# Layer 0's expert rows sorted over four batches instead of two, with raw rows loaded again and a new order of the work

## The reference, cut to what matters

```
xn = _layernorm(x)
x = x + _L0_attn_ref(xn, ...) + _L0_ffn_ref(xn, ...)     # layer 0
xn = _layernorm(x)
x = x + _L1_attn_ref(xn, ...) + _L1_ffn_ref(xn, ...)     # layer 1
```

```
logits = xf @ gate_w; scores = softmax(logits); top_scores, top_idx = top_k(scores, 2)
xs = scale.T[:, :, None] * xf[None]
h = silu(einsum('etd,edh->eth', xs, w1)) * einsum('etd,edh->eth', xs, w3)
out = einsum('eth,ehd->etd', h, w2).sum(axis=0)
```

## Time and profile before

| what | value |
|---|---|
| runs | 1793.97 us median of 3 (1791.5, 1793.97, 1795.19) |
| profiled execution, first to last instruction | 1782.7 us, 11.3 us less than the median run |
| of it layer 0 (to the barrier at 569.6 us) | 569.6 us |
| of it layer 1 | 1213.1 us |
| TensorE matmul busy, whole program | 1631.9 us (92%) |
| VectorE / ScalarE / GpSimd busy | 1494.5 (84%) / 1330.3 (75%) / 1353.8 (76%) us |
| DMA, whole program | 139 GB/s mean |

### The profile page before, as it was taken

The page is one execution under the profiler, slowest core; times in us unless marked ns, Lnnn a source line. Parts: engine busy times, 40 slices in busy tenths (PEclk is TensorE's granted clock), DMA queues, the critical chain, the costliest instruction groups (busy, mean ns, idle before and its releaser), DMA issues.

```text
span 1782.7 us, 44372 instructions
## 1 busy us (share of the span) xinstructions
PE 1631.9 (92%) x13580; PEld 1005.0 (56%) x13580; DVE 1494.5 (84%) x2798; ACT 1330.3 (75%) x3259; POOL 1353.8 (76%) x1114
## 2 busy tenths in 40 slices
PE   6999899899884888799999999999999999999988
PEld 4576585685673354355456456456556555544645
DVE  6848758668565999989989999999989999998997
ACT  4867666666652867968978987888897897797765
POOL 2807707618634078998999899899899999889996
PEclk9999999999996989999999999999999999999999
DMA  9446445645465843374373455446535446445430
GB/s 283 153 131 139 141 141 140 163 148 122 132 177 135 218 139 94 109 202 107 121 195 95 143 137 131 126 133 149 150 105 147 121 124 175 102 143 155 113 95 25
DMA packets 164993, 247.65 MB, mean 139 GB/s; under 512 B 30776, under 2 KB 109304, under 8 KB 164760
## 3 DMA queue, kind: packets, MB, share of 16 engines
q1 hardware_dynamic: 152472, 228.02, 45.9%
q0 software_dynamic: 12288, 16.79, 4.6%
HBM read 168.08 MB, written 73.50 MB: 136 GB/s over the span
## 4 chain that ended last, share of the span: by engine, by line
PE 31%; DVE 11%; issue 9%; ACT 8%; POOL 6%; DMA 2%; SPq 1%; DVEq 0%; POOLq 0%; ACTq 0%
PE bank L2323 28%; POOL HB L2274 3%; DVE bank L2846 3%; PE bank L2423 3%; DVE HB L2846 2%; POOL HB L2280 2%; DVE SU L2818 2%; ACT bank L2636 1%; ACT PR L2674 1%; DVE HB L2851 1%; ACT PT L2558 1%; DVE rows L2793 1%; DMA BC<-ssm_scratch 1%; ACT PR L2667 1%; PE bank L2451 1%
## 5 line engine op out<-in xcount | busy, mean ns | idle before, releaser
L2274 POOL TENSOR_TENSOR HB<-DD,BC 128x512 f32<-128x512 f32 x512 | 642.0, 1282 | 98.7 <-DMA DD<-SU 45.7
L2636 ACT ACTIVATE bank<-DD,A 128x512 f32<-128x512 f32 x512 | 349.6, 694 | 116.7 <-DVE HB L2851 74.2
L2280 POOL TENSOR_TENSOR HB<-HB,BC 128x512 f32<-128x512 f32 x256 | 324.9, 1285 | 31.2 <-DVE HB L2846 29.8
L2846 DVE TENSOR_TENSOR_SCAN bank<-bank,HB 128x512 f32<-128x512 f32 x256 | 310.7, 1214 | 23.5 <-ACT bank L2636 18.0
L2846 DVE TENSOR_TENSOR_SCAN HB<-bank,HB 128x512 f32<-128x512 f32 x256 | 309.8, 1210 | 7.8 <-ACT bank L2636 4.6
L2851 DVE TENSOR_TENSOR HB<-bank,BC 128x512 f32<-128x512 f32 x256 | 175.1, 684 | 15.9 <-DVE bank L2846 0.9
L692 POOL DMA_INDIRECT X<-expert_out_scratch,slot x64 | 111.1, 1736 | 66.2 <-DMA expert_out_scratch<-YS 39.4
L2323 PE MATMUL bank<-HB,fold 128*32 128x512 f32 x1024 | 137.0, 607 | 22.4 <-POOL HB L2280 10.9
L2423 PEld LDWEIGHTS bank<-ident,PR 128*128 128x128 f32 x768 | 86.7, 142 | 83.4 <-issue 44.9
L2423 PE MATMUL bank<-ident,PR 128*128 128x128 f32 x768 | 114.6, 281 | 18.8 <-ACT PR L2674 7.4
L2323 PE MATMUL bank<-XT,edge 128*128 128x512 f32 x256 | 122.7, 613 | 2.2 <-ACT XT L2558 2.0
(11 more groups left out here) (286 smaller groups left out, 3584.1 us busy)
## 6 DMA issues: line engine op xcount, KB each, us to landing
DD<-dd_scratch SPq DMA_DIRECT2D x488, 128.0 KB, 3.2
ROW<-row_scratch SPq DMA_DIRECT2D x64, 256.0 KB
BC<-ssm_scratch SPq DMA_DIRECT2D x128, 128.0 KB, 3.9
US<-us_scratch SPq DMA_DIRECT2D x32, 512.0 KB, 4.9
dd_scratch<-SU SPq DMA_DIRECT2D x16, 1024.0 KB, 5.5
us_scratch<-SU SPq DMA_DIRECT2D x15, 1024.0 KB, 6.5
XL<-sorted_scratch SPq DMA_DIRECT2D x92, 128.0 KB, 2.4
expert_out_scratch<-YS SPq DMA_DIRECT2D x92, 128.0 KB, 1.8
```

The costliest lines, as they stand in the source:

```text
L2274: done(pool.tensor_tensor(HB[:, c % HR], du, bc, ALU.mult), "dbu")
L2280: done(pool.tensor_tensor(h, h, bc, ALU.mult), "cg")
L2636: done(act.activation(PD[n % 2][:], delta, ACT.Exp, scale=A[:, k:k + 1]), "dA")
L2846: done(dve.tensor_tensor_scan(h if n % 2 else dA, dA, h, 0.0, ALU.mult, ALU.add), "scan")
```

## The change: larger groups, raw rows, attention first, a new table

The group grows to GB = 4 batches: TT = 16, MT = 39, two groups, 78 tiles. `MT` also sizes the zero fills. POOL's `sx` reads raw rows from a new buffer XR (loaded by the new SP step `xr`, 32 loads of 128 KB) and does the normalisation itself: subtract the mean, multiply by weight times rstd (`scaled`, a twelfth rank step). X has 3 slots for batches, XT 3; QT, KT, Q2, Q2T have 2 slots for tiles, not 4; XSC 4, not 8; XL 4, not 6. For batches 0 to 3 `ya` adds attention to raw x and the gather adds the expert rows behind it; for batches 4 to 7 it stays the other way round. `row_stats` and `x1_store` now wait for both. All of `L0_ORDER` is new.

```diff
-GB = 2
+GB = 4
 TT = GB * NT
 MT = 2 * TT + E - 1
+MTR = (MT + 1) // 2
-XNS, SXS, XLS, XSS, HSS, YSS = 2, 8, 6, 3, 3, 4
-RANKS = 11
+XNS, XTS, XS, XRS, SXS, XLS, XSS, HSS, YSS = 2, 3, 3, 3, 4, 4, 3, 3, 4
+RANKS, QS = 12, 2
+ATTENTION_FIRST = 4
...
+                def rows_load_raw(g, x):
+                    b, t = batch_tile(g, x)
+                    n = TT * g + x
+                    if n >= XRS:
+                        bb, xx = divmod(n - XRS, TT)
+                        after(sp, "sx", bb, 2 * xx, 2 * xx + 1)
+                    sp.dma_start(XR[:, n % XRS], x_rows(b, t)).then_inc(over[f"rows_in{n % XRS}"], 16)
...
                 def scaled_rows(g, i):
...
                     after(pool, "n", g, RANKS - 1)
-                    after(pool, "xn1", b, t)
+                    k = TT * g + x
+                    pool.wait_ge(over[f"rows_in{k % XRS}"], 16 * (k // XRS + 1))
...
-                    done(pool.tensor_scalar(XSC[:, n % SXS], XN1[:, b % XNS, t], weight[:, x, c:c + 1], None, ALU.mult), "sx")
+                    done(pool.tensor_scalar(XSC[:, n % SXS], XR[:, k % XRS], columns(mv1[:, :, 0], b)[:, t:t + 1],
+                                            scaled[:, x, c:c + 1], ALU.subtract, ALU.mult), "sx")
...
                 def add_expert_rows(g, i):
...
-                    pool.wait_ge(over[f"xx_in{x}"], 16 * (g + 1))
+                    if b < ATTENTION_FIRST:
+                        after(pool, "ya", b, t)
+                    else:
+                        rows_again_in(pool, b, t)
...
                 def add(b, t):
                     after(dve, "wo", b, t)
-                    g, x = group_tile(b, t)
-                    added(dve, b, t)
+                    if b < ATTENTION_FIRST:
+                        rows_again_in(dve, b, t)
+                    else:
+                        added(dve, b, t)
...
                 def x1_store(b, t):
                     after(sp, "ya", b, t)
+                    added(sp, b, t)
```

The new table, one line of each side:

```diff
-    "x_ld": [0, 22, 97, 270, 505, 988, 1329, 1719],
+    "x_ld": [0, 27, 63, 116, 279, 395, 460, 585],
```

More of the change, by code:

```diff
@@ L477, in sorted_in, with row_slot, rows_again_in, group_added @@
                 eng.wait_ge(moved[f"sort_in{r}"], 16 * (2 * TT // SXS) * (g + 1))
+        def row_slot(b, t):
+            return b % XS * NT + t
         def added(eng, b, t):
-            g, x = group_tile(b, t)
-            eng.wait_ge(moved[f"add{x}"], 32 * (g + 1))
+            eng.wait_ge(moved[f"add{row_slot(b, t)}"], 32 * (b // XS + 1))
+        def rows_again_in(eng, b, t):
+            eng.wait_ge(over[f"xx_in{row_slot(b, t)}"], 16 * (b // XS + 1))
+        def group_added(eng, g):
+            for b in range(GB * g, GB * (g + 1)):
+                for t in range(NT):
+                    added(eng, b, t)
         def tiles_moved(eng, name, slots, g):
@@ L548, in tile_store @@
                     after(sp, "yc", g, j)
-                    for x in range(TT):
-                        if g >= 2:
-                            sp.wait_ge(moved[f"add{x}"], 32 * (g - 1))
+                    if g >= 2:
+                        group_added(sp, g - 2)
                     m = MT * g + j
@@ L599, in _ @@
                         rows_load(b, i)
+                    elif what == "xr":
+                        rows_load_raw(b, i)
                     elif what == "ld":
@@ L615, in _ @@
                     sp.wait_ge(over[f"xn2_st{t}"], 16 * B)
-                for n in range(TT):
-                    sp.wait_ge(over[f"x1_st{n}"], 16 * B // GB)
+                for n in range(XS):
+                    sp.wait_ge(over[f"x1_st{n}"], 16 * NT * ((B - n + XS - 1) // XS))
                 sp.wait_ge(over["s_st"], 16 * B)
@@ L660, in input_rstd @@
                     after(pool, "agg", b, 0)
-                    after(pool, "xn1", b - 1, *range(NT))
-                    done(pool.tensor_tensor(rstd1[:], ve1[:], half[:, 0:NT], ALU.pow), "rs1")
+                    done(pool.tensor_tensor(columns(rstd1[:], b), ve1[:], half[:, 0:NT], ALU.pow), "rs1")
                 def scaled_rows(g, i):
@@ L947, in _ @@
                     elif what == "rg":
-                        weight_rows(b)
+                        weight_rows(b, i)
                     elif what == "tt":
@@ L1323, in rank_step @@
                     elif i == 9:
+                        q = dve.tensor_reduce(weight[:, :, 1], pick[:], X_AXIS, ALU.add)
+                    elif i == 10:
+                        q = dve.tensor_tensor(weight[:, :, 0], allw[:], weight[:, :, 1], ALU.subtract)
+                    else:
                         after(dve, "sx", g - 1, *range(2 * TT))
-                        q = dve.tensor_reduce(weight[:, :, 1], pick[:], X_AXIS, ALU.add)
-                    else:
-                        q = dve.tensor_tensor(weight[:, :, 0], allw[:], weight[:, :, 1], ALU.subtract)
+                        for c in range(GB):
+                            after(dve, "rs1", GB * g + c, 0)
+                        rates = rstd1[:, g * TT:(g + 1) * TT]
+                        q = dve.tensor_tensor(scaled[:], weight[:], bc(rates, 2), ALU.mult)
                     done(q, "n")
```

175 lines of the change are left out of this document (90 added, 85 removed), and 337 rows, old and new, of the table L0_ORDER.

## The result

The changed kernel took 1822.4 us (median of 4 runs) beside 1794.6 us for the kernel before: ratio 1.0155, 95% interval 1.0124 to 1.0187. A second comparison gave 1.0169 (1.0118 to 1.0221). So it is 28 us slower: slower was the likeliest of the three cases, but the time lies above the range (1768 to 1818).

A forecast was written before the change was run, and what follows sets the result against it. TensorE sets the pace in layer 0's long middle, POOL's chain and gathers its ends; 243 + 239 + 92 = 574 us against 569.6 (+4.4), so span 1787.1, plus 11.3 gives 1798.4 us, range 1768 to 1818.

The forecast's parts named there:

- the three cases: Whole time: faster (under 1790.4 us) 0.37, within 0.2% of no change 0.13, slower (over 1797.6) 0.50.
- Start: Layer 0's start: loads and zero fills ahead of ROW delay the first decay scan to 64 us, against 36.8.
- rival 1: Layer 0's start: ROW's loads get past the fills, first scan near 37 us, total 1771; chance 0.24.
- To the rank steps: First scan to first scaled tile: VectorE's 83 us of work at 0.9 takes 92 us, done at 156.
- The sort: POOL's 32 pairs before the first tile: 83 us, then 4, first tile at 243; second operation in `sx` adds nothing.
- Rival 3: POOL's sorts: two-operation `sx` costs 0.3 us more, each sort chain grows 10 us, total 1818; chance 0.10.
- First to last tile: Layer 0's expert tiles: TensorE's 227 us of queued work at 0.95 takes 239 us, ending at 482.
- No slack, no wait: Second group's sort begins some 21 us after the first tile, done at 108, just where TensorE wants its first tile.
- Fewer tiles: Layer 0's middle: 14 fewer tiles at 1.83 us each save 25.6 us of TensorE time, if TensorE still leads.
- Tail: Behind the last tile: 32 gathers and 16 powers on POOL lead, 92 us against 55.7, including 10.7 after the last gather.
- Layer 1: Code and order unchanged, so it stays at 1213.1 us; off by more than 3 would make the prediction wrong.
- Rival 4: SP's queue: `x1s` of batches 0 to 3 waits for gathers, holding tiles up 3 us each: +12, 1810; chance 0.10.

The follow-up runs named there:

- third series: Follow-up runs beside a kernel before of 1791.1 us: changed kernel again 1820.4, three repairs 1796.6, second operation in the kernel before 1811.9, its 19 tiles per group 1775.0.
- second series: Follow-up runs beside a kernel before of 1848.7 us: second operation in it 1855.1, its 19 tiles per group 1830.9; changed kernel with mean on VectorE 1833.2, three repairs 1809.8.

## Why the prediction was right and wrong, step by step

**Start: right.** Scan at 63.0 for 64, with the cause as given: with the fills out of the way it was at 42.4. (The parts as given, 57.4, 3.0 and at most 5.1, add up to 65.5; I took 64.) The Trainium skill's rule of ring order (DMA: Bandwidth & Descriptors, Queues, rings and completion order) agrees with these runs; rival 1 was wrong. What I had not priced is that SP's own issue stands still behind the fills (15.14 us), though the earlier trace rows had it with 8.83 and 10.36 us. TensorE then stood for 15.7 us, up to 69.8.

**To the rank steps: 12 us too long.** I gave VectorE 83 us of work between the scan and POOL's first scaled tile, at a rate of 0.9, and it took 81.3. By the trace it had 77.6 us of work there, a rate of 0.95, inside my bounds: one half of the error is work priced too high, the other the rate. From 80 to 144 us it was busy for 61.4 of 64.0 us.

**The sort: the failed step.** I took nothing for the second operation, "since it moves the same elements". It cost 0.31 us per instruction at the quickest, and 9.6 of the 14 us by which the first sort overran (97.4 us instead of 83; 87.9 with one operation). The remaining 4.9 us are not explained. The overrun used up the 12 us won before it; so the first tile at 245.9 (243 predicted) is right by two errors that cancel. Rival 3 priced this at 0.3 us, 10 us for each sort, and 1818; the run with one operation is 17 us faster, which would put the changed kernel near 1805, inside the forecast's own range of 1788 to 1808. Two operations in the old kernel are 21 us slower in the third series and 6 in the second. I gave the right mechanism 0.10. The number of elements was the wrong thing to reason from: with the same elements, the second operation added a third to the scaling's quickest time (1.22 against 0.91 us).

**First to last tile: 14 us too short.** "No slack, no wait" was on the edge. The second sort began 25 us in, not 21, took 88.3 us and was done 113 us in, not 108; with one operation it was done 103 us in and this stage took 243.8 us, near the 239. But TensorE waited only 5.4 us for tile loads within the stage, and with fills in parts, both operations and a granted clock of 0.98 instead of 0.96 it took 245.8 us. So the second operation is part of the cause; the clock may be another, and no run tells them apart.

**Fewer tiles: over-priced.** 14 tiles are worth 11 to 16 us at the 0.8 to 1.1 us that 16 of them won, not 25.6. The 1.83 us came from the fourth group, where no attention runs beside the tiles. Why a tile gives back less than it takes was not tested: waits for sorts and gathers that stay are one candidate, and the lower granted clock (0.96 instead of 0.98) is the other.

**Tail: the total 10 us short, and the reason wrong.** From the last tile's matmul to the end of the last gather it took 81.6 us, and I had predicted 81.5 (4.4 + 32 × 2.04 + 16 × 0.74), by luck: with half of the gathers gone the same stretch took 76.8. "Attention that is added last hides behind gathers, not the other way" was the wrong way round. What was short is the last term, from the last gather's end to the barrier: 20.9 us instead of 10.7. With layer 1's first loads issued sooner it was 15.5; the other 5 us are open.

**Layer 1: right**, 1215.7 against 1213.1, within the 3 us allowed. The 11.3 us that I added between span and median run were the kernel before's own spread and not a constant: the changed kernel's profiled execution was 1818.9 us with a span of 1817.1, 5.3 us under its median. So layer 0 came out 27 us too long, layer 1 added 3, and this term took back 6: 24 us over the forecast.

**Rival 4** (SP's queue) was not tested by itself. TensorE waited 14.2 us for XL in layer 0, 8.8 of it at the first tile, which leaves little for it.

## What to carry to other kernels

Price every added operation on an in-order engine that feeds others, even where the instruction count stays the same: a range "from nothing to a second pass" must enter the forecast and not only the rivals when the chain behind it has no slack. A bulk fill that nobody needs for 100 us does not belong ahead of a small store on the same queue. And that a resource's predicted time equals a stage's length doesn't show that it sets it; taking half of its work away does.

## What the runs showed of the hardware that I had not expected

- POOL's 128x256 scaling took 0.91 us at the quickest with one operation and 1.22 with two, and on the mean 1.01 and 1.43 us in the changed kernel. Six long cases (such as 4.80 us for two) each stand beside a decay scan of 2.3 us on VectorE. Whether they come from the port that both share, as the Trainium skill has it for a VectorE instruction with two inputs in SBUF (SBUF — State Buffer, Who interferes with whom), no run here shows, but the trace fits it.
- A queue full of zeros holds the issuing engine itself: 15.14 us for one small store behind two fills, 14.77 us for two fills in a row and 15.93 us for the two small loads behind those.
- In three of five series the kernel before took 1843 to 1849 us, at a mean granted clock of 0.962 to 0.965 instead of 0.974. For one and the same kernel (the one before with a second operation in its scaling), TensorE's waits for issue, in the runs of small matmuls, were 36.0 us in the second series and 18.3 in the third. Between its first and last tile TensorE was busy for 420.5 us there at a granted clock of 0.93, and for 398.7 us at 0.96 in the third. The row is of the slower series:

```profile
PE bank L718 <- issue: 36.0, 67, 2.7
```

  Versions of the change had 10.3 to 21.5 us of such waits in those series and 5.7 to 13.5 in the others. Whether waits or clock come first, and why the old order suffers more, isn't settled; the changed kernel itself didn't run in those series, so whether it would win there is likely from its variants (0.983 without 16 gathers) but not shown.
